# The first batch's score maxima in two halves, the second half inside the batch

## The chip, the cores and the metric

One core of one Trainium2 chip runs the kernel. The metric is the device time of one launch in microseconds (us). Five engines work side by side and meet only at semaphores: TensorE (PE: matmuls, and PEld: the loading of their weights), VectorE (DVE), ScalarE (ACT), GpSimd (POOL) and SyncE (SP), which here only issues DMAs. ACT and POOL issue DMAs too. Each engine takes its instructions in the order in which they are written for it.

## The reference, cut to what matters

```python
x = x + 0.5 * ffn(layernorm(x), ...)     # mixture of 8 experts, top 2
x = x + attention(layernorm(x), ...)
x = x + 0.5 * ffn(layernorm(x), ...)

# attention: x is (8 batches, 512 rows, 128), 16 heads of 8 columns
att = einsum('bhqd,bhkd->bhqk', q, k) / sqrt(8)
att = att + slopes[h] * (k_index - q_index)
att = softmax(where(causal, att, -inf), axis=-1)
y   = einsum('bhqk,bhkd->bhqd', att, v)
```

A softmax subtracts each row's largest score before the exponential. This kernel finds these maxima in a pass of its own and then computes the scores a second time, with the maximum already subtracted.

## The kernel before

The kernel has three stages: the first expert layer (`experts(0)`), the attention over eight batches (`over_batches`), and the second expert layer (`experts(1)`). The change lies where the first stage meets the second.

**Units.** The 16 heads of a batch are handled in four groups (`t`). A group has ten units, so a batch has 40, in two kinds of pass. The pass for the maxima (`scores_for_max` on PE) multiplies 128 queries by 128 keys of four heads at once into one of three PSUM banks (`ps_a`); where the block lies on the diagonal a second matmul adds the causal mask (four of ten units). `reduce_` on DVE takes the row maxima out of the bank and frees it. The second pass (`scores` on PE) writes a unit of 512 columns into one of two banks (`ps_b`), and `exp_` on ACT takes the exponential out of it into `arena`.

**From maxima to scores.** When 40 units are reduced, `maxima` on DVE reduces over the key blocks and splits the negated maxima into a high and a low part (four instructions, `mx` to `mx2`), `transpose_max` on PE turns them (four transposes into the bank `pair`), `maxima` on ACT copies them to `mT_zero`, and `maxima` on SP sends them by DMA into eight rows of the operand `qT`. `scores` then finds the subtraction in its own matmul. Its first unit waits for that DMA (`max_in`).

**The order.** Each engine's program lists the batch in 40 slots, one `scores` unit and one `exp_` to a slot. `beside(slot)` says which units of the *next* batch's maxima stand in a slot: four in slot 0, then about 1.1 per slot up to slot 33; `maxima` of the next batch stands in slot 34 on DVE and in slot 36 on PE and ACT. Batch 0 has no batch before it, so its own 40 units stand alone between `experts(0)` and batch 0. On ACT there stand, between the last expert work and batch 0: 16 DMAs of the second half of batch 0's operands (`operands(act, 0, 0, 1)`), the gate's tanh of chunk 2 (`gate_tanh(2)`, which waits for a sum that POOL makes in `sum_pairs(0, 2)`), and `maxima(0)`.

**The operands.** `operands(engine, b, u, h)` issues the 16 DMAs of one half (groups 0 and 1, or 2 and 3) of a batch's `qT` and `kZ`: one of zeros, three of queries, twelve of keys. SP issues both halves of the later batches: in batch 0 it issues the second half of batch 1, and then the first half of batch 2, which waits until `q_k_low(2)` on DVE (slot 26) has made the low parts. Behind it on SP stands `maxima(1)`. The units for batch 2's maxima, which stand in batch 1, read that first half.

The line numbers of the profile that the text uses: L2361 unit for the maxima, L2363 its mask, L1923 its reduction, L1929 to L1938 `maxima` on DVE, L2376 the transposes, L1332 the copy on ACT, L656 the DMA of the maxima, L2401 unit of the scores, L1326 its exponential, L2426 the product with the values, L585 to L595 the operands, L1181 the tanh, L885 to L908 POOL's sums, L1610 and L1612 `q_k_low`, L1408 to L1413 the statistics of a later batch.

## Time and profile before

| what | value |
|---|---|
| median of 3 runs | 887.24 us (885.19 to 888.77) |
| the profiled execution | 885.58 us |
| its span, first to last instruction | 883.8 us |
| around the span | 1.8 us |
| mean granted TensorE clock | 0.913 |
| busy: PE, PEld, DVE | 77%, 56%, 64% |
| busy: ACT, POOL | 46%, 55% |

All times of day below are microseconds from the start of the span. The chain of waits is the way back from the last instruction, at each step to what released it. In a timeline a bracket holds the idle time before an instruction and what ended it. A granted clock of 1.00 is 2.4 GHz and 0.50 is 1.2 GHz. Ends of matmuls are modelled, so the distance from start to start tells more than a duration.

### The profile page before, as it was taken

How to read it: one execution, taken by the hardware profiler on the slowest of the kernel's cores; microseconds unless marked ns; L12 is line 12 of the kernel's file. 1: busy time of each engine (PE TensorE's matmuls, PEld its weight loads, DVE VectorE, ACT ScalarE, POOL GpSimd, SP SyncE). 2: the span in 40 equal slices, each digit the busy share in tenths (PEclk: the TensorE clock that was granted, in tenths of full speed). 3: DMA queues.
4: the chain of work that ended last, by engine and by line, in shares of the span. 5: the costliest groups of instructions: out<-in, count | busy, mean ns of one | idle time of the engine just before them, and what ended most of it. 6: DMA issues, size and time to landing. Idle time of an engine off the chain costs nothing.

```text
span 883.8 us, 16149 instructions
## 1 busy us (share of the span) xinstructions
PE 683.1 (77%) x4719; PEld 492.3 (56%) x4719; DVE 568.2 (64%) x1922; ACT 410.8 (46%) x931; POOL 485.6 (55%) x588
## 2 busy tenths in 40 slices
PE   1465667979897798997988979999997777838760
PEld 1355656979793354654646545455544466837750
DVE  3675545968767876876767767787673235745538
ACT  2243411545560265664545645556554655615530
POOL 2656554034512666576866768373645466566661
PEclk9968777988898899998999999999997999969985
DMA  8614544744348313023050240302201235233525
GB/s 242 205 48 117 132 123 115 183 112 105 94 113 192 110 31 98 18 65 87 2 130 21 49 103 1 98 17 55 61 13 53 85 78 167 75 93 84 175 96 154
DMA packets 89825, 84.04 MB, mean 95 GB/s; under 512 B 14561, under 2 KB 72556, under 8 KB 89580
## 3 DMA queue, kind: packets, MB, share of 16 engines
q1 hardware_dynamic: 74472, 57.51, 25.8%
q0 software_dynamic: 8800, 19.72, 7.5%
q10 hardware_dynamic: 6468, 5.79, 2.8%
q8 instruction: 40, 0.66, 0.3%
q14 instruction: 45, 0.37, 0.1%
HBM read 43.84 MB, written 31.13 MB: 85 GB/s over the span
## 4 chain that ended last, share of the span: by engine, by line
PE 46%; DVE 15%; another core or an unknown queue 11%; issue 7%; ACT 7%; SPq 5%; ACTq 3%; DMA 3%; POOL 1%; DVEq 0%; POOLq 0%
PE bank L2361 6%; PE bank L2271 6%; PE bank L2401 6%; PE bank L2286 6%; PE bank L2426 6%; SPq L595 4%; DVE mx_of L1923 3%; PE pair L2449 2%; PE bank L2363 2%; ACT beside_parts L1254 2%; DMA qT<-mT_zero 2%; PE pair L2213 2%; PE bank L2246 1%; ACT arena L1326 1%
## 5 line engine op out<-in xcount | busy, mean ns | idle before, releaser
L1326 ACT ACTIVATE arena<-bank 128x512 f32<-128x512 f32 x320 | 184.0, 599 | 175.2 <-PE bank L2401 147.1
L1923 DVE TENSOR_REDUCE mx_of<-bank 128x4 f32<-128x512 f32 x320 | 204.2, 684 | 81.9 <-PE bank L2361 42.9
L2401 PE MATMUL bank<-qT,kZ 128*128 128x512 f32 (+3 forms) x512 | 156.9, 377 | 19.2 <-ACT arena L1326 12.4
L975 POOL TENSOR_SCALAR_AFFINE_SELECT arena<-arena 128x256 f32<-128x256 f32 (+1 forms) x192 | 95.4, 521 | 123.9 <-ACT arena L1326 122.5
L2361 PE MATMUL bank<-kZ,qT 128*128 128x512 f32 x320 | 148.5, 481 | 15.7 <-DVE mx_of L1923 6.2
L2401 PEld LDWEIGHTS bank<-qT,kZ 128*128 128x128 f32 x512 | 95.7, 197 | 49.2 <-ACT arena L1326 24.1
L868 POOL DMA_INDIRECT z_rows<-beside_kZ,place x80 | 78.7, 984 | 51.5 <-DVE place L1685 29.8
L2361 PEld LDWEIGHTS bank<-kZ,qT 128*128 128x128 f32 x320 | 63.1, 200 | 70.7 <-issue 31.4
L885 POOL DMA_INDIRECT sums<-y_rows,y_place x56 | 54.4, 971 | 84.9 <-DMA y_rows<-arena 70.0
L2426 PE MATMUL bank<-arena,vA 128*9 128x512 f32 (+3 forms) x1024 | 92.4, 440 | 5.2 <-POOL arena L975 2.7
L1254 ACT ACTIVATE beside_parts<-bank,hidden_bias 128x128 f32<-128x128 f32 x160 | 45.5, 381 | 69.6 <-remote 44.0
L2286 PE MATMUL bank<-w_rot,beside_parts 128*128 x320 | 51.2, 297 | 31.7 <-ACT beside_parts L1254 29.0
L1254 ACT ACTIVATE arena<-bank,hidden_bias 128x128 f32<-128x128 f32 x160 | 45.5, 371 | 48.7 <-PE bank L2271 33.4
L1799 DVE TENSOR_SCALAR arena<-bank,arena 128x132 f32<-128x132 f32 x128 | 39.3, 348 | 44.3 <-remote 25.1
L944 POOL DMA_INDIRECT y_rows<-arena x48 | 49.3, 1026 | 31.8 <-DVE arena L1799 20.5
L2286 PEld LDWEIGHTS bank<-w_rot,beside_parts 128*128 128x128 f32 x320 | 43.9, 197 | 36.2 <-issue 35.3
L2286 PE MATMUL bank<-w_rot,arena 128*128 x320 | 50.4, 295 | 7.0 <-issue 5.2
L868 POOL DMA_INDIRECT z_rows<-w,place x48 | 47.0, 979 | 13.4 <-issue 13.4
L2271 PE MATMUL bank<-beside_parts,beside_qT 128*128 128x128 f32 x320 | 46.6, 286 | 8.3 <-issue 5.1
L2363 PE MATMUL bank<-fixed,ident_bf 128*128 128x512 bf16 x128 | 52.5, 410 | 0.0
L2271 PE MATMUL bank<-arena 128*128 128x128 f32 x320 | 47.0, 291 | 3.8 <-DVE arena L1846 2.2
L2286 PEld LDWEIGHTS bank<-w_rot,arena 128*128 128x128 f32 x320 | 44.6, 200 | 9.0 <-issue 8.2
(286 smaller groups left out, 1306.7 us busy)
## 6 DMA issues: line engine op xcount, KB each, us to landing
arena<-z_rows SPq DMA_DIRECT2D x128, 66.0 KB
qT<-parts SPq DMA_DIRECT2D x42, 128.0 KB
kZ<-parts SPq DMA_DIRECT2D x168, 32.0 KB
y_rows<-arena SPq DMA_DIRECT2D x20, 264.0 KB, 3.3
kZ<-bias_k_r SPq DMA_DIRECT2D x8, 512.0 KB
beside_kZ<-y_rows SPq DMA_DIRECT2D x7, 528.0 KB, 3.9
z_rows<-in_spare SPq DMA_DIRECT2D x4, 528.0 KB
z_rows<-in_spare SPq DMA_DIRECT2D x32, 66.0 KB
```

The source lines that it names most:

```text
L868: g_.indirect_dma_start(z_rows[run], bass.IndirectOffsetOnAxis(place[g % DEEP][:, k, t:t + 1], 0), zz(g)[:, k, t, :], None).then_inc(z_sen ...
L885: g_.indirect_dma_start(terms(0, c)[0][:, t, k, :], None, y_rows[run], bass.IndirectOffsetOnAxis(y_place[:, c, k, t:t + 1], 0)).then_inc(s ...
L975: g_.affine_select(out=cut, in_=cut, compare_op=ALU.is_ge, fill=0.0, base=0, pattern=[[0, 2], [0, blocks], [1, P]], channel_multiplier=-1) ...
L1254: a_(hidden_rows(layer, p)[:, i, j, :], ps_up[p % 2][:, P * n:P * (n + 1)], ACT.Gelu, bias=hidden_bias[:, j, bass.ds(e, 1)]).then_inc(hidd ...
L1326: a_(dst, src, ACT.Exp).then_inc(exp_ok.sem, 1)
L1923: v.tensor_reduce(mx_of[:, queries, :, t, keys], ps_a[n % NA][:, :].rearrange("p (q n) -> p q n", q=NQ), AX.X, ALU.max).then_inc(reduced.s ...
L2271: last = mm(into, tile(w1_e, j), tile(turned_x(layer, q), t), start=True, stop=True)
L2286: mm(into, hidden_rows(layer, p)[:, i, j, :], w2_rot[:, bass.ds(e, 1), j, :].rearrange("p a n -> p (a n)"), start=(j == 0), stop=False)
L2361: last = mm(into, qT[u][:, t, P * queries:P * (queries + 1)], heads, start=True, stop=(queries != keys))
L2363: last = mm(into, ident_bf[:, :], mask_qk[:, :].unsqueeze(1).to_broadcast([P, NQ, P]), start=False, stop=True)
L2401: return mm(outp, kZ[u][:, h, lo:lo + P], qT[u][:, t, lo:SEQ], start=start, stop=True, skip_group_check=(kind != "full"))
L2426: last = mm(ps_o[32 * q:32 * q + HD + 1, kb * P:SEQ], vA[u][:, kb, NG * q + t, :], pT[t % 2][:, q, PT_KB[kb]:PT_KB[kb] + n], start=(kb == ...
```

## The change

The 40 units of batch 0's maxima are cut into two halves of 20 (groups 0 and 1, and groups 2 and 3). The first half stands alone as before; then `first_maxima(0)`, with half the rows, goes through DVE, PE, ACT and SP, and batch 0 begins. The other 20 units stand two by two in slots 0 to 9 of batch 0, `first_maxima(1)` follows in slot 9 on DVE and in slot 11 on PE and ACT. The 40 units for batch 1 move from slots 0 to 33 to slots 10 to 33, 1.67 to a slot instead of 1.1. `scores` waits for the second half's DMA only at unit 20. On SP the first half's DMA stands where the whole one stood; the second half's stands behind the second half of batch 1's operands, and a wait ahead of these keeps them until unit 20 of the maxima is computed. The semaphores of the four steps count one item more from then on (`LaterSteps`). The place of `gate_tanh(2)` on ACT is unchanged.

```diff
--- before.py
+++ after.py
@@ -108,6 +108,7 @@
 UNITS = 10
 N_UNITS = UNITS * NG
 A_SLOTS, A_FIRST = 34, 3
+FIRST_SLOTS, FIRST_HALF, AT_FIRST_MAX = 10, N_UNITS // 2, 11

 PT_KB = (0, 640, 1024, 512)
 PT_W = 1280
@@ -127,11 +128,19 @@
 assert len(MAX_UNITS) == UNITS


-def beside(slot):
+def beside(b, slot):

     def until(n):
-        return min(N_UNITS, A_FIRST + (N_UNITS - A_FIRST) * n // A_SLOTS)
-    return range(until(slot) if slot else 0, until(slot + 1))
+        if b == 0:
+            return max(0, N_UNITS * (n - FIRST_SLOTS) // (A_SLOTS - FIRST_SLOTS))
+        return A_FIRST + (N_UNITS - A_FIRST) * n // A_SLOTS
+    return range(min(N_UNITS, until(slot)) if slot else 0, min(N_UNITS, until(slot + 1)))
+
+
+def beside_first(slot):
+
+    n = FIRST_HALF + (N_UNITS - FIRST_HALF) // FIRST_SLOTS * slot
+    return range(n, n + (N_UNITS - FIRST_HALF) // FIRST_SLOTS) if slot < FIRST_SLOTS else range(0)


 def early(item, last):
@@ -148,6 +157,14 @@
     def value(self, item, step=None):

         return item * self.per + (self.per if step is None else step)
+
+
+class LaterSteps(Steps):
+
+
+    def value(self, item, step=None):
+
+        return super().value(item + 1, step)


 class Run:
@@ -357,6 +374,8 @@
         mx_of = sb("mx_of", [P, NT, NQ, NG, NT])
         mx_h = sb("mx_h", [P, NT, NQ, NG], FP32R)
         mx2 = sb("mx2", [P, NT, NQ, 2, NG])
+        mx2_half = mx2[:, :, :, :, :].rearrange("p i g a t -> p (i g a t)")[:, 0:2 * NT * NQ * HALF].rearrange(
+            "p (i g a t) -> p i g a t", i=NT, a=2, t=HALF)
         mT_zero = sb("mT_zero", [32 + 2 * NQ, SEQ], FP32R)
         mT, zeros_max = mT_zero[0:32, :], mT_zero[32:32 + 2 * NQ, :]
         v_next = sb("v_next", [P, SEQ])
@@ -496,10 +515,10 @@
         operands_in = [Steps(sem(f"operands_in{h}"), 16 * (3 + 3 * NQ + 1)) for h in range(2)]
         a_scores = Steps(sem("a_scores"), N_UNITS)
         reduced = Steps(sem("reduced"), N_UNITS)
-        max_split = Steps(sem("max_split"), 4)
-        max_transposed = Steps(sem("max_transposed"), 1)
-        max_rows = Steps(sem("max_rows"), 1)
-        max_in = Steps(sem("max_in"), 16)
+        max_split = LaterSteps(sem("max_split"), 4)
+        max_transposed = LaterSteps(sem("max_transposed"), 1)
+        max_rows = LaterSteps(sem("max_rows"), 1)
+        max_in = LaterSteps(sem("max_in"), 16)
         b_scores = Steps(sem("b_scores"), N_UNITS)
         exp_ok = Steps(sem("exp_ok"), N_UNITS)
         triangle_ok = Steps(sem("triangle_ok"), NG * MASK_OPS)
@@ -655,6 +674,12 @@
                 wait(sp, max_rows, b)
                 sp.dma_start(qT[u][ROW_MAX:ROW_MAX + 2 * NQ, :, :].bitcast(FP32),
                              mT.bitcast(FP32)).then_inc(max_in.sem, 16)
+
+            def first_maxima(half):
+
+                wait(sp, max_rows, half - 1)
+                sp.dma_start(qT[0][ROW_MAX:ROW_MAX + 2 * NQ, HALF * half:HALF * (half + 1), :].bitcast(FP32),
+                             mT[0:2 * NQ * HALF, :].bitcast(FP32)).then_inc(max_in.sem, 16)

             def load_abel_act(c):

@@ -762,13 +787,17 @@
             operands(sp, 1, 1, 0)
             for run in range(2, 4):
                 spare_rows(run)
-            maxima(0, 0)
+            first_maxima(0)

             def batch(b, u, first, later):
                 if b + 3 < BATCH:
                     load_abel_act(b + 3)
+                if first:
+                    wait(sp, a_scores, 0, FIRST_HALF + 1)
                 if later >= 1:
                     operands(sp, b + 1, 1 - u, 1)
+                if first:
+                    first_maxima(1)
                 if later == 2:
                     operands(sp, b + 2, u, 0)
                 if not first and later >= 1:
@@ -1325,6 +1354,12 @@
                     src = score_bank(b, n)[0][:, :].rearrange("p (h n) -> p h n", h=2)
                 a_(dst, src, ACT.Exp).then_inc(exp_ok.sem, 1)

+            def first_maxima(half):
+                wait(act, max_transposed, half - 1)
+                if half:
+                    wait(act, max_in, half - 2)
+                a_(mT[0:2 * NQ * HALF, :], ps_m[0][0:2 * NQ * HALF, :], ACT.Copy).then_inc(max_rows.sem, 1)
+
             def maxima(b):
                 wait(act, max_transposed, b)
                 if not early(b, 0):
@@ -1351,6 +1386,8 @@
             def batch(b, u, first, later):
                 for n in range(N_UNITS):
                     exp_(b, n)
+                    if first and n == AT_FIRST_MAX:
+                        first_maxima(1)
                     if n == AT_LAST_O and not first:
                         o_evac(b - 1, 3)
                     if n == (AT_Y if later else LAST_Y) and not first:
@@ -1385,7 +1422,7 @@
             experts(0)
             operands(act, 0, 0, 1)
             gate_tanh(2)
-            maxima(0)
+            first_maxima(0)
             over_batches(act, batch)
             experts(1)
             for c in range(CH):
@@ -1939,6 +1976,23 @@
                                                 ALU.mult, ALU.subtract))
                 run.end()

+            def first_maxima(half):
+                run = Run(dve, max_split, half - 1)
+                groups = slice(HALF * half, HALF * (half + 1))
+                wait(dve, reduced, 0, FIRST_HALF * (half + 1))
+                run.step(v.tensor_reduce(mx[:, :, :, groups].rearrange("p g q t -> p (g q) t"),
+                                         mx_of[:, :, :, groups, :].rearrange("p g q t k -> p (g q) t k"), AX.X, ALU.max))
+                run.join()
+                run.step(v.tensor_scalar(mx_h[:, :, :, groups], mx[:, :, :, groups], -1.0, None, ALU.mult))
+                run.join()
+                if half:
+                    wait(dve, max_transposed, half - 2)
+                mh = mx_h[:, :, :, groups].bitcast(FP32)
+                run.step(v.tensor_copy(mx2_half[:, :, :, 0, :], mh))
+                run.step(v.scalar_tensor_tensor(mx2_half[:, :, :, 1, :], mx[:, :, :, groups], -1.0, mh,
+                                                ALU.mult, ALU.subtract))
+                run.end()
+
             def normalise(b, i):

                 run = Run(dve, y_normalised, b)
@@ -1985,8 +2039,13 @@
                             x_low(b + 2)
                         if n == AT_LOW:
                             q_k_low(b + 2)
+                    if first:
+                        for a in beside_first(n):
+                            reduce_(0, a)
+                        if n == FIRST_SLOTS - 1:
+                            first_maxima(1)
                     if later >= 1:
-                        for a in beside(n):
+                        for a in beside(b, n):
                             reduce_(b + 1, a)
                         if n == AT_MAXIMA:
                             maxima(b + 1)
@@ -2041,9 +2100,9 @@
                         sum_pairs(1, 1)

             experts(0)
-            for n in range(N_UNITS):
+            for n in range(FIRST_HALF):
                 reduce_(0, n)
-            maxima(0)
+            first_maxima(0)
             over_batches(dve, batch)
             experts(1)
             for c in range(CH):
@@ -2377,12 +2436,25 @@
                                                mx2[:, i, :, :, :].rearrange("p g a t -> p (g a t)"), ident[:, :])
                 last.then_inc(max_transposed.sem, 1)

+            def first_transpose_max(half):
+                wait(pe, max_split, half - 1)
+                if half:
+                    wait(pe, max_rows, half - 2)
+                else:
+                    wait(pe, k_out, 1)
+                for i in range(NT):
+                    last = nc.tensor.transpose(ps_m[0][0:2 * NQ * HALF, i * P:(i + 1) * P],
+                                               mx2_half[:, i, :, :, :].rearrange("p g a t -> p (g a t)"), ident[:, :])
+                last.then_inc(max_transposed.sem, 1)
+
             def scores(b, u, n):

                 t, i = divmod(n, UNITS)
                 kind, q = list(units())[i]
                 bank_, ring = score_bank(b, n)
                 if n == 0:
+                    wait(pe, max_in, -1 if early(b, 0) else b)
+                if early(b, 0) and n == FIRST_HALF:
                     wait(pe, max_in, b)
                 if early(b, 0) and n < ring:
                     wait(pe, x_out, 0)
@@ -2464,8 +2536,13 @@
             def batch(b, u, first, later):
                 for n in range(N_UNITS):
                     t, i = divmod(n, UNITS)
+                    if first:
+                        for a in beside_first(n):
+                            scores_for_max(0, 0, a)
+                        if n == AT_FIRST_MAX:
+                            first_transpose_max(1)
                     if later >= 1:
-                        for a in beside(n):
+                        for a in beside(b, n):
                             scores_for_max(b + 1, 1 - u, a)
                     scores(b, u, n)
                     if not first:
@@ -2523,9 +2600,9 @@
                         ranks(2 * CH - 1)

             experts(0)
-            for n in range(N_UNITS):
+            for n in range(FIRST_HALF):
                 scores_for_max(0, 0, n)
-            transpose_max(0)
+            first_transpose_max(0)
             over_batches(pe, batch)
             experts(1)

```

How the order moves on DVE, from the last expert work into batch 0 (`arena<-bank` is an expert's output, `mx_of` a reduction, `mx` the maxima, `stat` to `var` the statistics of batch 2). Before, then now:

```order
L1799 TENSOR_SCALAR arena<-bank,arena 128x132 x2
L1923 TENSOR_REDUCE mx_of<-bank 128x4 x40
L1929 TENSOR_REDUCE mx<-mx_of 128x64
L1932 TENSOR_SCALAR mx_h<-mx 128x64
L1937 COPY mx<-mx_h 128x16x4
L1938 SCALAR_TENSOR_TENSOR mx<-mx,mx_h 128x16x4
L1923 TENSOR_REDUCE mx_of<-bank 128x4 x6
L1408 BN_STATS stat<-x_all 128x6 x4
L1411 BN_AGGR mv<-stat 128x2 x4
L1413 TENSOR_SCALAR var<-mv 128x4
L1923 TENSOR_REDUCE mx_of<-bank 128x4 x12
L1583 TENSOR_SCALAR work<-x_all,mv,rstd 128x128 x4
```

```order
L1960 TENSOR_REDUCE mx_of<-bank 128x4 x20
L1983 TENSOR_REDUCE mx<-mx_of 128x16x2
L1986 TENSOR_SCALAR mx_h<-mx 128x16x2
L1991 COPY mx<-mx_h 128x16x2
L1992 SCALAR_TENSOR_TENSOR mx<-mx,mx_h 128x16x2
L1960 TENSOR_REDUCE mx_of<-bank 128x4 x6
L1445 BN_STATS stat<-x_all 128x6 x4
L1448 BN_AGGR mv<-stat 128x2 x4
L1450 TENSOR_SCALAR var<-mv 128x4
L1960 TENSOR_REDUCE mx_of<-bank 128x4 x14
L1983 TENSOR_REDUCE mx<-mx_of 128x16x2
L1986 TENSOR_SCALAR mx_h<-mx 128x16x2
```

Of the 40 reductions ahead of batch 0, 20 have moved behind the first maxima; the four instructions of the maxima stand there twice, each on half the columns.

On ACT at the same place (`gate<-gate` is the tanh of chunk 2, `mT_zero` the copy of the maxima, `arena<-bank` an exponential), before and now:

```order
L595 DMA kZ<-oT 8x2x512 x4
L1181 ACTIVATE gate<-gate,cols 128x4
L1332 ACTIVATE mT_zero<-pair 32x512
L1326 ACT_TABLE_LOAD
L1326 ACTIVATE arena<-bank 128x512 x4
```

```order
L614 DMA kZ<-oT 8x2x512 x4
L1210 ACTIVATE gate<-gate,cols 128x4
L1361 ACTIVATE mT_zero<-pair 16x512
L1355 ACT_TABLE_LOAD
L1355 ACTIVATE arena<-bank 128x512 x4
L1355 ACTIVATE arena<-bank 128x2x256
L1355 ACTIVATE arena<-bank 128x512 x4
L1355 ACTIVATE arena<-bank 128x2x256
L1355 ACTIVATE arena<-bank 128x512 x2
L1361 ACTIVATE mT_zero<-pair 16x512
```

The copy of the maxima has become a copy of half the rows behind the same tanh, and a second one stands behind the exponentials of slots 0 to 11.

## Rows read from the trace of the kernel before

**Rows 1.** The page: shares of the chain of waits by engine.

```profile
PE 46%; DVE 15%; another core or an unknown queue 11%; issue 7%; ACT 7%; SPq 5%; ACTq 3%; DMA 3%; POOL 1%; DVEq 0%; POOLq 0%
```

**Rows 2.** Busy time by stretch: the columns stand in the first line.

```profile
core 0: us, PE busy (x) PEld busy (x) DVE busy (x) ACT busy (x) POOL busy (x), PEclk, DMA share, GB/s
283.00:289.30 6.30, 6.22 (x14) 3.21 (x14) 5.05 (x8) 0.00 (x0) 4.78 (x6) 0.50 0.69 187
289.30:296.70 7.40, 5.57 (x16) 2.24 (x14) 7.38 (x13) 0.30 (x1) 3.88 (x6) 1.00 0.30 101
347.30:350.00 2.70, 2.67 (x7) 1.49 (x7) 1.65 (x3) 0.00 (x0) 2.22 (x3) 0.50 0.73 191
...
314.00:332.30 18.30, 18.30 (x125) 10.34 (x123) 13.10 (x23) 11.95 (x23) 13.41 (x20) 1.00 0.03 7
```

**Rows 3.** Chain of waits into batch 0: start, length, what.

```profile
289.43 7.28 DVE mx_of L1923 x12
296.73 0.43 DVE mx L1929
...
299.45 1.03 PE pair L2376 x4
300.50 0.59 ACT mT_zero L1332
301.11 2.92 DMA qT<-mT_zero
...
304.24 0.50 PE bank L2401
```

**Rows 4.** Timeline, ACT ahead of batch 0: start, length, what, idle before.

```profile
295.44 0.30 ACT L1181 ACTIVATE gate<-gate,cols 128x4 f32<-128x4 f32 x1 [28.95 <-POOL gate L897]
```

**Rows 5.** Timeline, DVE, PE and SP between the two halves of the units.

```profile
269.28 12.05 DVE L1923 TENSOR_REDUCE mx_of<-bank 128x4 f32<-128x512 f32 x20 [0.65 <-PE bank L2361]
...
283.08 1.22 PE L2361 MATMUL bank<-kZ,qT 128*128 128x512 f32 x2 [2.99 <-DMA kZ<-oT]
...
286.76 1.26 SPq L638 DMA_DIRECT2D z_rows<-in_spare  x2
```

**Rows 6.** Timeline, DVE in batch 0: statistics, then batch 1's maxima.

```profile
306.22 0.86 DVE L1408 BATCH_NORM_STATS2 stat<-x_all 128x6 f32<-128x128 f32 x4
...
307.64 0.17 DVE L1413 TENSOR_SCALAR var<-mv 128x4 f32<-128x4 f32 x1
...
329.77 1.29 DVE L1923 TENSOR_REDUCE mx_of<-bank 128x4 f32<-128x512 f32 x2 [2.16 <-PE bank L2363]
...
340.85 0.42 DVE L1929 TENSOR_REDUCE mx<-mx_of 128x64 f32<-128x256 f32 x1
...
342.29 0.49 DVE L1938 SCALAR_TENSOR_TENSOR mx<-mx,mx_h 128x64 f32<-128x64 f32 x1
```

**Rows 7.** Chain of waits in batch 0 and into batch 1.

```profile
322.73 0.23 PE bank L2361
322.96 0.23 PE bank L2363
...
334.30 0.70 SPq L585
...
344.77 2.51 DMA kZ<-parts
...
347.33 1.22 PE bank L2361 x2
```

**Rows 8.** Timeline, PE and SP in batch 0 and at its end.

```profile
310.74 0.50 PE L2401 MATMUL bank<-qT,kZ 128*128 128x512 f32 x1 [1.18 <-issue]
...
313.80 0.62 PE L2361 MATMUL bank<-kZ,qT 128*128 128x512 f32 x2
...
345.49 0.67 SPq L656 DMA_DIRECT2D qT<-mT_zero  x1
...
349.75 0.99 PE L2401 MATMUL bank<-qT,kZ 128*128 128x512 f32 x1
```

## The prediction

> **What bounds the kernel now.** I read the page first, then the chain of waits, the busy time by stretch, and last the timelines of the stretch that the change touches. The page's chain lies on PE for 46% and on DVE for 15% of the span [rows 1], so no engine bounds the whole; the place decides. The change touches 269 to 355 us, and the reader should see three things there.
>
> First, into batch 0 the chain is a plain sequence. DVE reduces the last units at 0.607 us each (7.28 / 12), then come the maxima on DVE from 296.73, the transposes at 299.45, ACT's copy at 300.50 and the DMA of 2.92 us from 301.11; the first scores start at 304.24 [rows 3]. From the end of the reductions that is 7.5 us in which no score is computed, and the change wants that time.
>
> Second, two more things stand in that stretch. The second half's units wait for their operands until 283.08 [rows 5]. And ACT, which must copy the maxima, waits 28.95 us for POOL's sum and runs the tanh of chunk 2 at 295.44, right behind that sum (L897) [rows 4]. The copy stands behind that tanh. In the kernel before this costs nothing, since the maxima come later (300.50).
>
> Third, inside batch 0 PE is full: from 314.0 to 332.3 it is busy 18.30 of 18.30 us at clock 1.00 while DVE is busy 13.10 [rows 2], and where DVE stops it waits for PE (2.16 us at 329.77) [rows 6]. The batch ends on another chain: `q_k_low` on DVE releases SP at 334.30, which issues 16 DMAs, the last one lands 2.51 us after 344.77, and PE starts on batch 2's units at 347.33 [rows 7]. Whatever moves `q_k_low` of slot 26 moves batch 1.
>
> **The change part by part.** *The start of batch 0.* The first half's 20 units are reduced at 281.33 (269.28 + 12.05) [rows 5]; its maxima and transposes are over by about 284, in the shadow of the wait for operands. Then ACT cannot copy before its tanh is done: 295.44 + 0.30 = 295.74. Copy 0.59 (296.33), DMA 2.92 (299.25), 0.20 to the first matmul: 299.45 instead of 304.24, a gain of 4.8 us. SP is free at 286.76 + 1.26 = 288.0 [rows 5], so it does not hold the DMA. The DMA carries half the bytes; the nearest DMA of that size took 2.51 us [rows 7], so the gain lies between 4.8 and 5.2, and I take 4.8 since its form is that of L656.
>
> *What PE and DVE do until then.* Units 20 and 21 stand ahead of the first scores and run from 283.08. Unit 22 stands behind them on PE, so 18 units (18 x 0.607 = 10.9 us of DVE) no longer run between 285 and 297, under the cover of POOL's sum; they run in the batch. This is the price of the change, and the order shows it: 20 reductions have moved behind the first maxima.
>
> *Slots 0 to 9.* DVE holds the pace: two reductions take 1.21 us a slot, PE needs about 3.8 matmuls of 0.23 (two units, 0.8 masks, one score), 0.9 us. From the first scores to the first of these reductions about 1.15 us (score and unit at half clock, then DVE's start): 300.6. Then 18 reductions 10.9; the statistics 1.6 (306.22 to 307.81) [rows 6]; the second half-maxima, which PE waits for in slot 11, 1.6; its transposes 0.6. The half-maxima have no row: the whole ones took 340.85 to 342.78, 1.93 us [rows 6], half of that is 0.97, and 296.73 to 299.45, 2.7 [rows 3], is the most. I take 1.6, nearer to the first, as four short dependent instructions shrink little. Sum: 300.6 + 14.7 = 315.3. PE will have been idle some 14 us, and after shorter waits it worked at half clock: 6.30 us from 283.0 (0.50), 2.70 us from 347.3 (0.50) [rows 2]. With 4.5 us, the mean of the two, some 2.6 slots lack 0.43 us each (3.8 x 0.43 = 1.64 against 1.21): 1.1 us. PE comes to slot 11 at 316.4; before it was there at 313.80 [rows 8]. The 4.8 gained have become 2.6 lost. A stall of 1.18 us in the old slots [rows 8] is not in this sum; if it stays, it adds up to 1.2.
>
> *Slots 11 to 25.* PE has 25 units here instead of 17, with 10 masks instead of 6: 12 matmuls more at 0.234 (0.23 each in the chain) [rows 7] = 2.8 us on an engine without idle time [rows 2]. DVE's sum (25 x 0.607 and 2 us of other work = 17.2) stays below PE's 21. So `q_k_low` and SP's 334.30 come 2.6 + 2.8 = 5.4 later: 339.7. The bounds are 0, if the stretch hides slack, and 8 x 0.607 + 2.8 = 7.7, if the units also stall on the three banks. The Trainium skill (TensorE: Matmul & The Clock Gate, Back-to-back issue gap) gives about 131 ns for a matmul of 512 columns in a stream; by that the 12 would cost 1.6 us and the whole change 1.2 us less than my sum. This trace shows 230 ns from start to start, so I go by the row.
>
> *The end of batch 0.* SP's DMAs run for 11.2 us (334.30 to 345.49 [rows 7, 8]) and land at 347.33 + 5.4 = 352.7. DVE has 14 reductions after `q_k_low` instead of 9: maxima at 339.7 + 14 x 0.607 = 348.2, done at 350.1 (1.93), transposes and copy 1.2 (351.3), SP free at 350.9, DMA 2.92 and 0.2: the first scores of batch 1 at 354.4. PE starts on batch 2's units at 352.7 with hardly an idle gap, so at full clock: 4 units and 2 masks take 1.4 us, not the 2.42 of before (347.33 to 349.75 [rows 7, 8]), and are done in time. The first scores were at 349.75 [rows 8]: 4.6 us later.
>
> *Edits at no cost.* The `wait` for unit 20 on SP is met at about 284, before SP stands there. The second half's DMA stands behind 16 DMAs from about 299.5 to 311 and its copy is ready at 317; unit 20 of the scores needs it past 325. The first half's copy, 16 rows instead of 32, is as long as its columns. The batches behind are a chain without a gap that would absorb a shift, so I carry the 4.6 to the end.
>
> **The sum.** 885.58 (the profiled execution: span 883.8 and 1.8 around it) + 4.6 = 890.2. That execution lies 1.66 below the median of the runs; on the median the same step gives 887.24 + 4.6 = **891.8 us**, which I forecast. About 0.5% (4.4 us) is what a measurement of this kernel can tell from no change, and the forecast lies just past that edge.
>
> **The rivals.** *The added matmuls are hidden, so not slower.* If the full stretch of 314 to 332 holds slack that a modelled end hides, the 2.8 us fall away: + 1.8, 889.0. For it: DVE's idle time there is no more than a fraction, and busy shares count modelled ends [rows 2]. Against it: starts 0.23 apart, with no wait between [rows 7], and DVE waiting 2.16 us for PE [rows 6]. It decides if the starts of matmuls in slots 11 to 25 come closer than 0.23 or the stretch takes under 19 us. With the skill's figure for the same step, above, the time would be 890.6.
>
> *The batch begins as soon as the half is in, so faster.* If POOL's L897 came by 284, ACT's copy would run at once, the DMA would go out when SP is free at 288.0 and the scores would start at 291.1, 8.3 us earlier than in my sum: 883.5. Against it: L897 waits for gathers whose landing the change does not touch, and ACT waited 28.95 us for it [rows 4].
>
> *Half clock through all ten slots, so much slower.* DVE sets PE's pace there, and PE waits between units. If the clock stayed at 0.50, slots 0 to 9 would take 10 x 0.43 = 4.3 us more instead of 1.1: 891.8 + 3.2 = 895.0. For it: 6.30 us at 0.50 in the same pattern of units [rows 2]. Against it: from 289.3 to 296.7 the same pattern ran at 1.00 with DVE busy 7.38 of 7.40 us, so PE's waits between units did not keep the clock down [rows 2].
>
> **How the numbers follow.** Forecast 0.48 (its own range 889 to 894.5, from the stall of 1.2 on one side, the cheaper DMA and half-maxima on the other), hidden matmuls 0.25, half clock 0.12, early copy 0.07, none of these 0.08. The range from 887.0 to 897.0 takes in the rival without the matmuls and the one at half clock with the stall, and leaves out the early copy and half of the unnamed rest. Of the forecast a little over half lies past the edge of 891.7, and all of the half clock: slower 0.45; the rest of the forecast and the hidden matmuls: same 0.46; faster 0.09.
>
> **What would show it.** In the changed profile: ACT's copy of 16 rows right behind the tanh at about 295.7, and PE without work from about 285 to 299 (the first step); DVE with hardly an idle time from 300 to 316 and PE in slot 11 at 316 to 317.5 (the second); SP's first DMA of batch 2's operands at about 339.7 instead of 334.3 (the third); the first scores of batch 1 at about 354.4 (the fourth), and from there the same distances as before. The prediction is wrong if the copy comes before 290, if SP's DMAs start before 336, or if batches 1 to 7 take up the shift.

## The result and the profile after

The changed kernel took 896.82 us (median, 896.7 to 901.38) against 888.0 us for the kernel before in the same runs: a ratio of 1.0094, 95% interval 1.005 to 1.0138. It is slower, by 8.3 us (0.0094 x 888.0; 4.4 to 12.3). The forecast was 891.8 us, 4.6 above the median that it started from, in a range of 887.0 to 897.0: sign and range hold, but the loss is nearly twice the forecast one. The question for the experiments is which step of the sum was too small.

The profiled execution of the changed kernel spans 894.7 us (before 883.8). Shares of its chain of waits, from the page, beside [rows 1]:

```profile
PE 46%; DVE 17%; another core or an unknown queue 9%; issue 7%; SPq 6%; ACT 5%; DMA 4%; POOL 3%; ACTq 2%; DVEq 0%; POOLq 0%
```

As a whole they tell little: DVE has gained 2 points, PE none. The place tells more. First ACT ahead of batch 0, beside [rows 4], and DVE and PE there (timeline: start, length, what, idle before):

```profile
279.91 0.29 DVE L1983 TENSOR_REDUCE mx<-mx_of 128x32 f32<-128x128 f32 x1
...
293.35 0.30 ACT L1210 ACTIVATE gate<-gate,cols 128x4 f32<-128x4 f32 x1 [28.30 <-POOL gate L926]
293.55 0.57 ACT L1361 ACTIVATE mT_zero<-pair 16x512 fp32r<-16x512 f32 x1
...
296.55 0.79 PE L2473 MATMUL bank<-qT,kZ 128*128 128x512 f32 x1 [14.12 <-DMA qT<-mT_zero]
```

The first half's maxima are formed at 279.91, and behind its transposes and units 20 and 21 PE and DVE stand until ACT has done its tanh and the copy has gone out. PE is idle for 14.12 us, and its first matmul of 512 columns takes 0.79 us, where the one at 310.74 before took 0.50 [rows 8]. Then the chain from there to batch 1, beside [rows 3, 7]:

```profile
293.55 0.58 ACT mT_zero L1361
294.15 2.36 DMA qT<-mT_zero
296.55 0.79 PE bank L2473
...
306.73 0.69 DVE mx_of L1960
307.42 2.12 another core or an unknown queue
309.56 0.70 DVE mx_of L1960
...
314.76 0.30 DVE mx L1983
...
316.25 1.02 PE pair L2446 x4
317.28 0.43 PE bank L2420
...
342.26 0.70 SPq L604
...
354.41 3.35 DMA qT<-mT_zero
357.80 0.50 PE bank L2473
```

The reader sees slots 0 to 9 from 296.55 to 317.28 (20.73 us, before 9.56 from 304.24 [rows 3] to 313.80 [rows 8]), with a wait of 2.12 us in them for which the trace names nothing on this core, and slots 11 to 25 from 317.28 to SP's 342.26 (24.98 us, before 20.50 [rows 7, 8]). Busy time by stretch, beside [rows 2]:

```profile
core 0: us, PE busy (x) PEld busy (x) DVE busy (x) ACT busy (x) POOL busy (x), PEclk, DMA share, GB/s
296.50:306.90 10.40, 10.03 (x29) 6.05 (x29) 7.76 (x20) 3.58 (x6) 7.49 (x9) 0.70 0.44 120
306.90:317.30 10.40, 6.91 (x19) 4.05 (x19) 7.05 (x13) 2.88 (x5) 4.51 (x8) 0.63 0.15 37
317.30:342.20 24.90, 24.38 (x144) 14.00 (x143) 18.88 (x33) 13.12 (x25) 13.08 (x19) 0.95 0.01 2
```

DVE, which was to be busy all the time in these slots, is busy 7.76 and 7.05 of 10.40 us. The granted clocks of 0.70 and 0.63 are means over its two levels. Cut where it changes, with PE's wait at the second change (busy time by stretch, then timeline):

```profile
296.50:302.60 6.10, 6.05 (x16) 4.03 (x16) 4.16 (x14) 2.05 (x4) 4.41 (x5) 0.50 0.44 119
302.60:309.50 6.90, 4.72 (x17) 2.32 (x16) 4.12 (x8) 1.54 (x3) 5.34 (x8) 0.99 0.47 125
309.50:319.50 10.00, 8.38 (x24) 5.15 (x24) 7.82 (x14) 3.23 (x6) 3.69 (x5) 0.51 0.02 5
```

```profile
310.31 0.79 PE L2420 MATMUL bank<-kZ,qT 128*128 128x512 f32 x1 [2.10 <-DVE mx_of L1960]
```

PE runs at half clock (1.2 GHz) for 6.10 us after the long wait, then at full clock, and at half clock again for some 10 us once it has stood still for 2.10 us.

**One origin for all runs.** The work ahead of batch 0 ends at another time in each execution, also where nothing was edited (the origin used below lies at 264.35 and 261.11 in two traces of the changed kernel). So the places are told from here on as microseconds after ACT's first operand DMA `qT<-mT_zero` (265.80 in the trace before, 264.35 in the one after). "Second transposes" are those of the second half (L2446 here), "operands" is SP's first DMA of batch 2 (342.26 here), "batch 1" its first scores (357.80). Each place comes from one profiled execution, the last column from all the runs of a kernel.

| kernel | first scores | second transposes | operands | batch 1 | ratio to before, interval |
|---|---|---|---|---|---|
| before | 38.4 | | 68.5 | 83.9 | 1 |
| changed | 32.2 | 51.9 | 77.9 | 93.4 | 1.0094, 1.005 to 1.0138 |
| changed, again | 31.9 | 50.6 | 74.9 | 90.3 | 1.0081, 1.0056 to 1.0107 |
| tanh later | 27.0 | 48.8 | 74.7 | 90.2 | 1.0104, 1.0051 to 1.0158 |
| before, tanh later | 37.4 | | 76.5 | 91.6 | 1.0086, 1.0052 to 1.0121 |
| operands late | 32.5 | 48.2 | 73.2 | 88.6 | 1.0066, 1.0032 to 1.01 |
| halves only | 34.1 | 34.5 | 69.0 | 84.1 | 1.0038, 1.0003 to 1.0072 |
| halves, early DMAs | 34.7 | 35.0 | 68.0 | 82.6 | 1.0016, 0.999 to 1.0042 |
| before, early DMAs | 36.0 | | 65.9 | 81.3 | 0.9986, 0.9955 to 1.0017 |
| changed, early DMAs | 34.4 | 50.0 | 74.4 | 89.8 | 1.0092, 1.0061 to 1.0122 |
| halves, early copy | 32.0 | 32.4 | 65.0 | 79.7 | 0.9973, 0.9944 to 1.0002 |
| ten units moved | 35.7 | 46.1 | 70.5 | 85.4 | 1.0044, 1.0016 to 1.0073 |
| PE kept busy | 31.2 | 48.3 | 73.7 | 89.2 | 1.0078, 1.005 to 1.0106 |
| ten moved, early copy | 24.2 | 38.1 | 66.8 | 82.1 | 1.0018, 0.999 to 1.0046 |

Two things are read from it at once. The time follows the column of batch 1 (the five kernels with the earliest starts there, up to 83.9, are the five fastest, and the seven rows that start at 88 or later are the seven slowest), so what was lost before batch 1 is kept to the end. And it doesn't follow the first column: the earliest first scores of all (24.2) end no better than the kernel before.

### The profile page after: what moved, and what is told of

Same layout as the page of the kernel before. It is cut to its first block, busy times and chain, and to the rows that moved or that the text cites. A ratio compares the mean times of both kernels' runs of the same rounds, so it can differ in the third digit from the quotient of the medians.

```text
span 894.7 us, 16168 instructions
## 1 busy us (share of the span) xinstructions
PE 689.3 (77%) x4723; PEld 501.3 (56%) x4723; DVE 567.5 (63%) x1926; ACT 411.4 (46%) x932; POOL 483.2 (54%) x588
## 4 chain that ended last, share of the span: by engine, by line
PE 46%; DVE 17%; another core or an unknown queue 9%; issue 7%; SPq 6%; ACT 5%; DMA 4%; POOL 3%; ACTq 2%; DVEq 0%; POOLq 0%
PE bank L2473 6%; PE bank L2420 6%; PE bank L2330 6%; PE bank L2345 6%; PE bank L2498 6%; SPq L614 4%; DVE mx_of L1960 3%; DMA qT<-mT_zero 2%; PE pair L2521 2%; PE bank L2422 2%; PE pair L2272 2%; PE bank L2185 1%; PE bank L2305 1%; PE bank L2184 1%
## 5 line engine op out<-in xcount | busy, mean ns | idle before, releaser
L914 POOL DMA_INDIRECT sums<-y_rows,y_place x56 | 54.5, 974 | 82.1 <-DMA y_rows<-arena 67.3
L2345 PE MATMUL bank<-w_rot,beside_parts 128*128 x320 | 55.2, 313 | 23.2 <-ACT beside_parts L1283 20.7
L2345 PEld LDWEIGHTS bank<-w_rot,beside_parts 128*128 128x128 f32 x320 | 48.1, 214 | 26.8 <-issue 25.8
L2330 PE MATMUL bank<-beside_parts,beside_qT 128*128 128x128 f32 x320 | 49.1, 297 | 10.5 <-issue 6.7
L2330 PEld LDWEIGHTS bank<-beside_parts,beside_qT 128*128 128x128 f32 x320 | 42.8, 206 | 13.1 <-issue 9.7
```

The lines of the kernel that those rows point to most:

```text
L914: g_.indirect_dma_start(terms(0, c)[0][:, t, k, :], None, y_rows[run], bass.IndirectOffsetOnAxis(y_place[:, c, k, t:t + 1], 0)).then_inc(s ...
L2330: last = mm(into, tile(w1_e, j), tile(turned_x(layer, q), t), start=True, stop=True)
L2345: mm(into, hidden_rows(layer, p)[:, i, j, :], w2_rot[:, bass.ds(e, 1), j, :].rearrange("p a n -> p (a n)"), start=(j == 0), stop=False)
```

## The experiments

The theory after the result: the moved units cost what DVE and PE need for them in the batch, and a wait beside the operand DMAs and a lower clock come on top. The rivals: the copy behind ACT's tanh, which lets a gain of 8 us lie unused; the halves themselves; the DMAs.

**The changed kernel once more**, unedited, for the size of the effect and the scatter of the places.

> The changed kernel itself, unedited, so that it stands beside the experiments on the same chip. Both theories expect its ratio to the kernel before again, 1.005 to 1.014; below 1.003 the first result would have been the luck of a few runs.

It took 890.45 us against 882.63, ratio 1.0081: 7.1 us (4.9 to 9.4). The loss is there again and above the forecast 4.6, though the places differ from the first trace by up to 3 us. The wait stands at the same reductions of DVE (timeline: start, length, what, idle before):

```profile
302.58 2.81 SPq L614 DMA_DIRECT2D kZ<-parts  x4
...
305.22 3.32 DVE L1960 TENSOR_REDUCE mx_of<-bank 128x4 f32<-128x512 f32 x5 [2.13 <-remote]
...
305.98 1.09 ACT L1355 ACTIVATE arena<-bank 128x512 f32<-128x512 f32 x2 [3.67 <-remote]
```

DVE and ACT both go on within 0.6 us of the time at which SP's 16 operand DMAs have been issued (302.58 + 2.81 = 305.39), and no engine of this core is named as what they waited for. "Remote" is the trace's word for a release that it can't place.

**The tanh in slot 2**, so that the copy comes as soon as the half's transposes are done; in the changed kernel and, beside it, in the kernel before.

```diff
+AT_TANH_2 = 2
...
+                    if first and n == AT_TANH_2:
+                        gate_tanh(2)
...
-            gate_tanh(2)
```

> The changed kernel with one edit: the tanh of chunk 2 on ACT moves from ahead of the first half's copy to slot 2 of batch 0. Theory A (the copy is held by the tanh, and what the batch loses later is a fixed price): the copy runs at about 283 instead of 293.55, the DMA goes out when SP is free (286.3), the first scores start at 289 to 292 instead of 296.55, and the whole gain of 5 to 7 us stays: 890 to 892 us. Theory B (the end of batch 0 is set by the sum of PE's and DVE's work from 283 on, and the half clock): the scores start as early as in A, but the ten slots run on at half clock, less than 3 us of it stay: 894 to 897. Theory C (another wait holds the copy): the first scores stay at 296.

> The kernel before with the tanh of chunk 2 moved to slot 2 of batch 0, nothing else. In the kernel before the copy of the maxima waits for the transposes at 300.50 and the tanh is done at 295.74, so theory A says that nothing changes: 886 to 889 us, first scores at 304 as before. If the tanh itself or POOL's sums behind it matter for the batch, the time moves by 2 us or more.

The changed kernel with it took 891.36 us (ratio 1.0104), so the earlier copy gained nothing in the time. (The 891.36 lies in theory A's range only since the kernel before took 881.88 in these runs, not 888.0.) The first scores came 4.9 us earlier than in the repeat (27.0 for 31.9) and the second transposes only 1.8 (48.8 for 50.6). The edit moves more than the copy: the tanh ran 2.7 us later than in the repeat (31.4 for 28.7 after the origin), and DVE's statistics of batch 2 need POOL's `x_all`, which stands behind that tanh. The gain went into this wait of DVE and into waits of ACT (timelines of DVE and ACT):

```profile
295.71 0.87 DVE L1447 BATCH_NORM_STATS2 stat<-x_all 128x6 f32<-128x128 f32 x4 [3.12 <-POOL x_all L938]
...
299.21 0.60 ACT L1356 ACTIVATE arena<-bank 128x512 f32<-128x512 f32 x1 [4.79 <-issue]
...
308.06 0.60 ACT L1356 ACTIVATE arena<-bank 128x512 f32<-128x512 f32 x1 [2.50 <-remote]
```

Slots 0 to 9 lasted 21.8 us from first scores to second transposes, where the repeat took 18.7. In the kernel before the same edit alone cost 7.6 us (0.0086 x 882), which shows that more than the copy waits for the tanh: DVE's statistics (3.31 us for POOL's `x_all`), and POOL itself (timeline):

```profile
305.32 0.19 POOL L904 TENSOR_SCALAR gate<-gate 128x4 f32<-128x4 f32 x1 [10.42 <-ACT gate L1182]
...
318.60 2.79 POOL L976 TENSOR_SCALAR_AFFINE_SELECT arena<-arena 128x256 f32<-128x256 f32 x6
```

POOL waits 10.42 us for the tanh, then issues eight gathers at 1.26 us from start to start, and only then masks batch 0's first triangle (318.60), without which PE has no first values (56.1 after the origin; in the trace before 49.6).

**SP's operands held back** until all 40 units are scored, so that their DMAs don't run beside slots 0 to 9.

```diff
-                    wait(sp, a_scores, 0, FIRST_HALF + 1)
+                    wait(sp, a_scores, 0, N_UNITS)
```

> The changed kernel with one edit: SP issues the second half of batch 1's operands only when unit 39 of batch 0's maxima is computed (about 313) instead of unit 20 (at once, 297.7 to 309.0). Theory A (the stall of 2.1 us at 307.4 in slots 5 to 6, in which ACT and DVE wait for nothing on the core, comes from these DMAs, and the clock falls to half because of it): the stall of 307 to 310 goes, the clock stays at 1.00 through slots 6 to 11, slot 11 starts 3 to 4 us earlier, and the time is 892 to 894. Theory B (the stall belongs to the place in the program): the stall stays at 307 to 310 and the time is within 1.5 us of 896.8.

No "remote" wait is left in these slots (the longest without a name is one of 1.37 us on PE, put down to "issue"). From first scores to second transposes they took 15.65 us, against 18.7 in the repeat and 19.7 in the first trace. The time came down to 1.0066, 5.8 us over the kernel before (2.8 to 8.8). Of the 3 us or more that the slots gained, batch 1 kept 1.7 (88.6 for 90.3). The difference in time to the repeat, 1.3 us, lies inside the intervals; the length of the slots is what this run shows.

**The halves without the move**: all 40 units ahead of batch 0 as before, the first half's transposes behind unit 22, the second half's in slot 1.

```diff
-            for n in range(FIRST_HALF):
+            for n in range(N_UNITS):
+                if n == FIRST_HALF + AHEAD:
+                    first_transpose_max(0)
                 scores_for_max(0, 0, n)
-            first_transpose_max(0)
```

> The halves without the move: all 40 units of batch 0's maxima stand ahead of the batch as in the kernel before, the first half's maxima go out in the middle of them (transposes behind unit 22), the second half's transposes and copy stand in slot 1, and batch 1's units stand as in the kernel before. Theory A (the price of the change is the 18 units that leave the cover of POOL's sum): the first scores start at 296 to 297, right behind unit 39 and the DMA, the batch carries no more units than before, SP's operands of batch 2 start 5 to 7 us earlier than in the kernel before, and the time is 5 to 7 us under it: 881 to 883. Theory B (the wait of 16 DMAs of operands or instruction loads in the first slots takes the gain, whatever stands beside): the time is within 2 us of the kernel before, 886 to 889.

884.75 us, ratio 1.0038, nothing gained: the first scores came 4.4 us earlier than before and the operands 0.5 later (69.0 for 68.5). Halving the maxima brings no gain by itself, and it leaves about half of the 7 to 8 us to the move; the next three runs measure that part. The waits are here too, with no unit moved: up to 2.13 us on DVE and 3.60 on ACT, both "remote".

**The move, with SP's operand DMAs ahead of the batch.** In the three kernels SP issues batch 1's second operands right behind the first ones, ahead of the first scores, and two copies of spare rows go behind batch 1's maxima. Between the last two of the following texts the place of 20 units differs, and what hangs on it: the transposes of both halves and the slots of batch 1's units (0 to 33, or 10 to 33).

```diff
-            for run in range(2, 4):
-                spare_rows(run)
+            wait(sp, a_scores, 0, N_UNITS // 2 + 1)
+            operands(sp, 1, 1, 1)
...
-                if later >= 1:
+                if later >= 1 and not first:
...
+                if first:
+                    for run in range(2, 4):
+                        spare_rows(run)
```

> The kernel before with the same edit on SP, nothing else. Theory A: the short stall in its slots 4 to 6 goes too, SP's operands of batch 2 start at 66 to 67 instead of 68.5 us after ACT's first operand DMA, and the time is 1 to 3 us under the kernel before. Theory B: no change, within 1 us.

> The halves without the move (all 40 units ahead of the batch), with one edit more on SP: the 16 DMAs of the second half of batch 1's operands go out right behind those of the first half, at about 285 to 296 while ACT waits, instead of into the first slots of batch 0, and the two copies of spare rows go behind batch 1's maxima. Theory A (these DMAs cause the stalls of 2 to 4 us in slots 1 to 4, in which ACT and DVE wait for nothing on the core): no such stall is left in the first ten slots, the first scores start about 34.5 us after ACT's first operand DMA as without the edit, SP's operands of batch 2 start at 64 to 66 instead of 69.0 us after it, and the time is 2 to 5 us under the kernel before. Theory B (the stalls belong to the place in the program): SP's operands of batch 2 start at 69 again, and the time is that of the kernel before or above.

> The changed kernel with the same edit on SP. The first half's maxima wait some 2 us for SP here, so the first scores start at 34 instead of 32.2 us after ACT's first operand DMA. Theory A: the stall in slots 5 to 6 goes, the second half's transposes come at 49 to 50 instead of 51.9, SP's operands of batch 2 at 73 to 75 instead of 77.9, and the time is 2 to 4 us under the changed kernel, but still 3 us or more above the kernel before, since the 18 units stay in the batch. Theory B (the DMAs cost nothing, the units everything): it is the changed kernel's time or 2 us more.

The kernel before with it took 880.95 us (ratio 0.9986), the halves 884.22 (1.0016), the changed kernel 890.84 (1.0092). The move, with the units of batch 1 that it pushes back, is worth 6.6 us in the medians (890.84 - 884.22), and 6.4 at the operands (74.4 for 68.0). The halves missed what was expected of them (operands at 64 to 66). The wait without a name is still there, though SP's operand DMAs were all issued by 32.3 after the origin (293.9; timelines of POOL, ACT and DVE):

```profile
302.98 0.95 POOL L907 DMA_INDIRECT sums<-y_rows,y_place  x1 [0.30 <-issue]
...
304.98 0.60 ACT L1348 ACTIVATE arena<-bank 128x512 f32<-128x512 f32 x1 [2.25 <-remote]
...
305.71 1.89 DVE L1953 TENSOR_REDUCE mx_of<-bank 128x4 f32<-128x512 f32 x3 [2.16 <-remote]
```

DVE and the busy time by stretch of the changed kernel with early DMAs:

```profile
304.70 8.46 DVE L1961 TENSOR_REDUCE mx_of<-bank 128x4 f32<-128x512 f32 x14
```

```profile
core 0: us, PE busy (x) PEld busy (x) DVE busy (x) ACT busy (x) POOL busy (x), PEclk, DMA share, GB/s
298.90:314.54 15.64, 12.90 (x43) 7.66 (x44) 13.59 (x31) 6.46 (x11) 8.70 (x13) 0.86 0.18 46
314.54:338.94 24.40, 23.88 (x148) 13.71 (x148) 19.54 (x34) 13.22 (x26) 13.79 (x19) 1.00 0.01 2
```

Fourteen reductions in a row without a pause (0.604 each): here DVE sets the pace, as the prediction had it, and the "remote" wait is gone. Behind the second transposes PE is busy 23.88 of 24.40 us at full clock: that stretch is PE's. Yet the kernel is no faster than the repeat, since the half's DMA now stands behind the operand DMAs on SP and the first scores start 2.5 us later (34.4 for 31.9).

**Ten units moved instead of twenty**, one in each of slots 0 to 9, with early DMAs; the first half's transposes stand behind unit 22.

```diff
-    n = FIRST_HALF + (N_UNITS - FIRST_HALF) // FIRST_SLOTS * slot
-    return range(n, n + (N_UNITS - FIRST_HALF) // FIRST_SLOTS) if slot < FIRST_SLOTS else range(0)
+    n = ALONE + (N_UNITS - ALONE) // FIRST_SLOTS * slot
+    return range(n, n + (N_UNITS - ALONE) // FIRST_SLOTS) if slot < FIRST_SLOTS else range(0)
```

> The changed kernel with batch 2's operands issued early, but only ten units (30 to 39) moved into slots 0 to 9, one in each; units 20 to 29 stay ahead of the batch. Theory (each moved unit costs its own matmul and reduction in the batch, about 0.33 us): SP's operands of batch 2 at about +71 us after ACT's first operand DMA, half way between +68.0 with none moved and +74.4 with twenty; time 887 to 888, 0.4 to 0.6% over the kernel before. Rival (the price comes only where two reductions stand in a slot and make DVE the pace): operands at +68 to +69 and time within 0.2% of the kernel before. Second rival (any move costs the same, through the wait for the second half): +74.

886.89 us, ratio 1.0044, operands at 70.5: near the number of the theory, but not for its reason. The stretches (busy time):

```profile
core 0: us, PE busy (x) PEld busy (x) DVE busy (x) ACT busy (x) POOL busy (x), PEclk, DMA share, GB/s
299.86:310.20 10.34, 8.50 (x31) 5.39 (x32) 8.02 (x22) 6.06 (x11) 6.56 (x11) 0.86 0.17 38
310.20:334.61 24.41, 23.90 (x148) 13.72 (x148) 19.55 (x34) 13.34 (x26) 14.22 (x20) 1.00 0.01 2
```

The stretch behind the second transposes is as long as with twenty (24.41 and 24.40), since batch 1's units start in slot 10 in both. All of the difference lies in slots 0 to 9: 10.34 for 15.64, 5.3 us or 0.53 for each unit (4.0 are left at the operands, since the first scores came 1.3 us later than with twenty). From the first scores to the operands it takes 33.3 us with no unit moved, of which some 2 are the wait shown above, 34.8 with ten and 40.0 with twenty: most of the price comes with the second ten. So the price has two parts that the total can't tell apart: nearly a whole reduction (0.604) for each unit that puts a second one into a slot, and the matmuls of batch 1 that are pushed into slots 11 to 25.

**PE kept busy** ahead of the first scores by 44 matmuls that belong to no result.

```diff
+WARM = 44
...
+                    if first and n == 0:
+                        for _ in range(WARM):
+                            mm(ps_o[:, :], ident_bf[:, :], mask_qk[:, :].unsqueeze(1).to_broadcast([P, NQ, P]), start=True, stop=True)
```

> The changed kernel with 44 matmuls that belong to no result, put on PE ahead of batch 0's first scores, so that PE does not idle while the copy and its DMA run. Theory (part of the loss is the half clock at which PE comes out of its idle time): the granted clock from the first scores on is 1.00 instead of 0.70, slots 0 to 9 get 1 to 2 us shorter, time 1 to 2 us under the changed kernel, still 0.5 to 0.9% over the kernel before. Rival (DVE sets the pace of the slots and PE's clock there decides nothing): slots 0 to 9 within 0.4 us of the changed kernel and the same time.

Busy time by stretch:

```profile
core 0: us, PE busy (x) PEld busy (x) DVE busy (x) ACT busy (x) POOL busy (x), PEclk, DMA share, GB/s
293.40:303.80 10.40, 8.90 (x34) 4.86 (x33) 8.78 (x22) 4.20 (x7) 7.49 (x9) 1.00 0.44 120
303.80:314.00 10.20, 7.51 (x23) 4.60 (x23) 7.33 (x14) 2.96 (x6) 5.97 (x9) 0.67 0.14 36
```

The clock of the first five slots is 1.00 (0.70 in the changed kernel), and slots 0 to 9 take 17.1 us for 18.7 in the repeat. So the low clock after the wait costs at most 1.6 us in these slots: the "remote" wait of DVE is not in this trace either, though SP's operand DMAs run beside the slots. The 0.67 is a mean again, and the clock falls behind a shorter wait of PE (timeline, busy time by stretch):

```profile
306.46 0.79 PE L2421 MATMUL bank<-kZ,qT 128*128 128x512 f32 x1 [1.32 <-DVE mx_of L1961]
```

```profile
306.40:312.00 5.60, 4.72 (x14) 2.77 (x14) 4.65 (x10) 2.28 (x4) 2.64 (x4) 0.50 0.02 6
```

The stretch from the second transposes to batch 2's operands took 25.4 us for 24.4, at a clock of 0.95 for 1.00, and the time is that of the changed kernel (1.0078 and 1.0081). The 1 to 2 us expected in the time are not seen: they are too small for these intervals, or are given back.

**The halves with an early copy**: all 40 units ahead of the batch, early DMAs, the half's DMA ahead of the second ones, the copy ahead of the tanh, and one unit of batch 1 instead of four ahead of the first scores (the expectation says none, but the edit leaves one there).

```diff
-            gate_tanh(2)
             first_maxima(0)
+            gate_tanh(2)
...
+        if b == 0:
+            return N_UNITS * n // A_SLOTS
```

> The maxima in halves with all 40 units ahead of batch 0, batch 2's operands issued early, and now also: ACT copies the first half before its tanh, SP issues the first half's DMA ahead of the long operand issues, and no unit of batch 1 stands in front of batch 0's first scores. Theory (the price of the changed kernel is the 20 units in the batch; where they stay under cover the halves themselves are worth what the chain into batch 0 gets shorter): first scores at +30 to +32 us after ACT's first operand DMA (halves with early operands: +34.7), SP's operands of batch 2 at +62 to +65 (there +68.0, kernel before +68.5), time 0.3 to 0.6% under the kernel before. Rival (the start of batch 0 is not what decides; stalls and the clock take the early start back): operands at +66 to +68, time as the kernel before within 0.2%.

880.26 us, ratio 0.9973: the lowest of all, 9.5 us below the changed kernel's repeat (0.0108 x 882), but its interval (0.9944 to 1.0002) still touches no change, so that it beats the kernel before is not shown. The operands came at 65.0, in the range given. The early copy does not decide the start here (timelines of ACT and PE):

```profile
284.30 0.59 ACT L1356 ACTIVATE mT_zero<-pair 16x512 fp32r<-16x512 f32 x1 [19.06 <-issue]
...
296.06 0.64 PE L2413 MATMUL bank<-kZ,qT 128*128 128x512 f32 x1 [1.38 <-DVE mx_of L1955]
296.50 0.63 PE L2466 MATMUL bank<-qT,kZ 128*128 128x512 f32 x1
```

The copy is at 284.30, and the first scores still stand at 296.50. The matmul at 296.06 is the unit of batch 1 that was left in front of them: it waits until DVE has reduced all 40 units of batch 0, the last of which PE started at 294.18. How early the first scores could come without it, this run does not show.

**Ten units moved, and the early copy.** If an early start pays at all, it should here, where the units moved are those that hold the first scores up.

```diff
             operands(sp, 1, 1, 0)
+            first_maxima(0)
             wait(sp, a_scores, 0, N_UNITS // 2 + 1)
             operands(sp, 1, 1, 1)
-            first_maxima(0)
...
-            gate_tanh(2)
             first_maxima(0)
+            gate_tanh(2)
```

> Ten units moved into slots 0 to 9, as in the run with ten, and the first half's copy ahead of ACT's tanh and its DMA ahead of the long operand issues, as in the run with the early copy: the two are put together. Theory (a move pays where the batch really begins earlier by it: ten units less of 0.607 us in front, against about 0.25 to 0.33 us for each in the batch): first scores at +26 to +27 us after ACT's first operand DMA, SP's operands of batch 2 at +61 to +63 (with all 40 units ahead and the early copy: +65.0), time 0.5 to 0.8% under the kernel before. Rival (what starts early waits in the batch for the same things: the second half, instruction stalls beside the operand DMAs, half clock): operands at +65 to +67, time within 0.3% of the kernel before.

883.87 us, ratio 1.0018, operands at 66.8: the rival's numbers, and the theory's gain did not come. The first scores came at 24.2, 2 us earlier than expected and 11.5 earlier than with ten units and the late copy; 3.7 of these are left at the operands (66.8 for 70.5), and the intervals of the two ratios overlap. Timelines of PE, DVE and POOL:

```profile
289.77 0.80 PE L2476 MATMUL bank<-qT,kZ 128*128 128x512 f32 x1 [2.43 <-ACT arena L1356]
...
291.36 0.87 DVE L1446 BATCH_NORM_STATS2 stat<-x_all 128x6 f32<-128x128 f32 x4 [2.93 <-POOL x_all L938]
...
300.96 0.95 POOL L915 DMA_INDIRECT sums<-y_rows,y_place  x1 [0.30 <-issue]
301.93 2.78 POOL L1005 TENSOR_SCALAR_AFFINE_SELECT arena<-arena 128x256 f32<-128x256 f32 x6
...
303.83 1.05 PE L2501 MATMUL bank<-arena,vA 128*9 128x512 f32 x8 [2.36 <-issue]
```

PE scores the first banks and then waits for ACT, whose exponentials stand behind the tanh that waits for POOL's sum (the tanh is at 287.51). DVE's statistics wait 2.93 us for what POOL makes behind it. Later the triangle stands behind POOL's gathers of the next chunk (the last at 300.96), and the first values come as soon as the first masks are out. What starts earlier thus meets POOL's program, which is as late as with the late copy (the last gather ends at 41.4 after the origin, there at 40.9). The stretch behind the second transposes grew to 28.7 us (24.4 with ten units and the late copy).

## Why the prediction was right in sign and too small

The sign held, and so did the four steps in kind. That the range held owes something to luck: 896.82 lies 0.2 us below its upper end, and outside the forecast's own range of 889 to 894.5. The terms named for that own range do not give its ends either: with the stall it is 893.0 (891.8 + 1.2), with the cheaper DMA (0.4) and half-maxima (0.6) 890.8.

**The first step** had the mechanism and too small a gain. The copy stands behind the tanh as forecast (293.35, 293.55). The first scores came 6.2 us earlier than before (32.2 for 38.4; 6.6 in the repeat), not 4.8 and beyond the bound of 5.2. Of the 1.4 us more, 0.6 are POOL's: the tanh came at 29.0 after the origin, before at 29.6 (295.44 [rows 4] less 265.80). Another 0.56 is the DMA (2.36 us for 2.92 [rows 3]), to which the nearest row of 2.51 [rows 7] had pointed; and the copy overlaps the tanh's end by 0.1.

**The second step is the mis-sized term.** The prediction let DVE go through slots 0 to 9 in 15.25 us (1.15 + 10.9 + 1.6 + 1.6) and 1.1 more for the clock, 16.35 from the first scores to the second transposes. The first trace took 19.7, the repeat 18.7. Where the operand DMAs are out of these slots, it is 15.65 (operands late) and 15.64 (early DMAs): with the pace that DVE sets, the sum was right to 0.7 us. Its parts were too: the half-maxima took 1.44 us (314.76 to 316.20) for 1.6. What failed is the sentence that put the stall of 1.18 us [rows 8] outside the sum as "up to 1.2". In the changed kernel the wait is 2.1 us on DVE and up to 3.7 on ACT. In the two runs that move SP's operand DMAs out of these slots it is absent, and they are 3.1 to 4.0 us shorter (15.65 for 18.7 or 19.7); the half clock behind the wait is part of that. That the added work made the stall larger is not shown: with no unit moved it was 2.13 and 3.60 us (halves only). The rival of half clock through all ten slots was right for about half of their time, but not in its reason. The clock rose after 6.1 us (6.0 in the repeat), where the sum had 4.5, and it fell again only when PE had stood still for 2.1 us, which the sum did not hold. Where it was lifted to 1.00 in the first half of these slots, they got only 1.6 us shorter, near the 1.1 of the sum and far from the rival's 4.3.

**The third step** held. The stretch from slot 11 to the operands took 23.8 us in the repeat and with early DMAs (from PE's first unit behind the second transposes in the chain of waits) for 20.3 before (313.96 to 334.30 in its chain), which is 3.4 more against the forecast 2.8 for 12 matmuls at 0.234 us [rows 7]; the profile counts 148 matmuls there with a busy share of 0.98. The rival that hides the matmuls falls: its sign was a stretch of under 19 us or starts closer than 0.23. The figure of the Trainium skill (TensorE: Matmul & The Clock Gate, Back-to-back issue gap), by which the 12 would cost an estimated 1.6 us, is not borne out here: matmuls of 512 columns start 0.23 us apart in this stretch, as before. The first trace took 4.5 us more than before; its clock was 0.95 in the stretch for 1.00 in the repeat, so the half clock of the second step reached into it (to 319.50).

**The fourth step** held in kind. PE went into batch 1 almost without an idle gap (0.64 us): from SP's operands to the first scores it took 15.5 us where the forecast had 14.7 and before 15.4, and the first scores' matmul took 0.50 us for 0.99 [rows 8]. The shift at batch 1 was 9.5 us in the first trace and 6.3 in the repeat, for 4.6; the times moved by 8.3 and 7.1. Batches behind didn't absorb it. With the operands held back, so that only what the sum contained was left, the shift was 4.6 us (88.6 for 83.9, from the unrounded 88.59 and 83.95), the forecast number, with 5.8 in the time. That the number agrees is luck in part: the first scores came 1.1 us earlier than forecast and slots 0 to 9 were 0.7 shorter, while the stretch behind them was 1.1 longer (25.0 for 23.9) and the end 0.7 (15.4 for 14.7).

**The early-copy rival** was worth a chance of 0.07 and less than that: the run with the copy before the tanh began the batch 4.9 us earlier and ended where the changed kernel does. That run also put off the tanh; where it was not put off, with ten units moved, a start 14 us earlier than before left the time as it was. The rival's error was to carry an early start through to the end with nothing in the batch that could take it back; the tanh, POOL's `x_all` for DVE's statistics, its gathers and its triangle do.

**Open.** What ends the waits that the trace puts down to "remote" or "issue" was not settled. In the changed kernel the "remote" ones are gone in both runs that move SP's operand DMAs out of slots 0 to 9, which speaks for the DMAs. Against them speaks that waits of 2.16 us on DVE and 2.25 on ACT stayed in the halves with early DMAs, and of 1.45 and 1.84 us with ten units and the early copy, though the operand DMAs were all issued some 10 us before; and with PE kept busy the DMAs ran beside the slots without such a wait on DVE. A rival that no run tests is the end of POOL's gathers. In all seven traces with a "remote" wait on DVE in these slots the last of the eight gathers ends inside such a wait (in microseconds after the origin: at 43.4 in 43.1 to 45.2 in the first trace, at 42.4 in 42.0 to 44.1 in the halves with early DMAs, at 54.2 in 52.4 to 55.9 in the kernel before with the tanh later); but other traces have the gathers without the wait. Nor is the first trace's larger loss explained beyond its clock.

## What to carry to other kernels

Work that stands under another engine's wait cost next to nothing here (with early DMAs the first scores came at 34.7 with all 40 units ahead, at 34.4 with 20); moved behind that wait it costs its time on the engine that then sets the pace (here 0.53 us for each unit that put a second reduction into its slot), and what it displaces costs again in the next stretch (some 3 us), together more than the 6 us by which the batch began earlier. Before moving work to start a batch earlier, follow each engine that the batch's first instructions need (here ACT behind a tanh behind POOL, DVE's statistics behind POOL's `x_all`, and POOL's masks behind its gathers), since an early start is only worth what the latest of them lets through. And a stall that stands in the slots which get the added work belongs into the sum, not beside it: here it came out at 2.1 to 3.7 us where up to 1.2 had been allowed. A mean clock between the two levels hides when it changed; cut the stretch finer before a cause is read from it.

## What the runs showed of the hardware

After an idle time of 14.12 us PE came back at half its clock, 1.2 GHz (0.79 us for a matmul that takes 0.50 at full clock; granted 0.50 over 6.10 us, then 0.99 over 6.90), while in the kernel before the clock was 1.00 when batch 0 began. Giving PE other matmuls in the idle time brought 1.00 there. But short waits were followed by half clock too: after PE had stood still for 2.10 us it was granted 0.51 over the next 10.00 us, though busy for 8.38 of them, and with PE kept busy, after a wait of 1.32 us, 0.50 over 5.60 us, busy for 4.72. And an early start of batch 0 by 14 us (24.2 for 38.4) changed the time of the whole kernel by less than 0.5%.
